# The last head group of an attention kernel gets a program of its own

## The chip, the cores and the metric

The kernel runs on one core of a Trainium2 chip. Five engines work at the same time, each with its own instruction stream, taken in order: TensorE (PE, matrix products), VectorE (DVE), ScalarE (ACT, activation functions), GpSimd (POOL) and SyncE (SP, which here issues every transfer). They are ordered against each other by semaphores alone. The metric is the device time of one execution in microseconds (us); the median of several runs is compared. The profile's span runs from the first to the last instruction of one profiled execution.

## The reference

The inputs are x of 8 x 1024 x 256, four 256 x 256 attention weights and three integer feed-forward weights of hidden size 768. With 16 heads of width 16:

```
xn = layernorm(x)
Q, K, V = xn wq, xn wk, xn wv          # 16 heads; rope on Q and K
probs = softmax(causal(Q K^T / sqrt(16)))
s = (probs V) wo
g = silu(ffn(xn, w_gate, w_up, w_down))
out = x + s * g
```

## The kernel before

The program has two phases. The first (some 480 us) computes Q, K, V and the gate g for all batches and puts them in memory. The second, attention, is what the change touches. It goes over 8 batches b and NG = 4 groups g of GH = 4 heads: 32 steps (b, g). The Python loop writes every step out, and a step is one period of a hand-written order, so that step n works on three things at once: the exponentials of step n, the maxima of steps n+1 and n+2, and the output tiles of a batch that is finished.

- Scores (`keys_by_queries`, L1189 in the trace): NU = 20 units u, each two banks of scores for one block of 128 keys; `EXPU` lists key block, first query, width and heads. ACT makes the exponential of each (`exponentials`, L1110) into one of four buffers `pr`. POOL zeroes the part above the diagonal for the 12 units in `diag_units` (`mask`, L974).
- `times_v(step, s)` (L1207): 12 products s of probabilities and V, four for the first half of the queries (c = 0), eight for the second. Products 9 to 11 (`late`) of a step are run in the period of the next. ACT copies each half of the result out (`take_output`, L1117), PE transposes it (`transpose_output`, L1227), and DVE divides by the row sums (`normalise`, L1060 and L1062) into `an`.
- Maxima (`queries_by_keys`, L1167 and L1175, and `maximum` on DVE, L1029). The last period has none, and that before it only those of the last step.
- Output tiles: 128 queries of a batch by 256, eight to a batch (QB). For each, POOL splits `an` into two half-precision parts (`split_tile`, L982 and L984), PE transposes them (`transpose_tile`, L1235), ACT takes them to `aT` (`take_tile`, L1122), PE multiplies by wo (`project_tile`, L1243, six products), ACT takes the result (`take_product`, L1128), and POOL multiplies by the gate and adds x (`add_tile`, L992 and L995). A full period does two tiles, through one bank, M0.

`ps` is the eight banks of PSUM: three slots of two banks for scores and maxima (`SLOTS`), one bank O0 for the products with V, and M0. `ORDER` is a string of 39 turns of PE; an E is a score unit, an M a unit of maxima, and turn t uses slot t mod 3 (`slot_of`, `wait_slot`). The tuples `V_AT`, `TR`, `WO`, `OUT0`, `OUT1` say behind which turn PE does the rest; `TAKE0`, `TAKE1`, `EV`, `MUL` do so for ACT, `HALVE` and `ADD` for POOL, by units.

When the 32 periods are over, nine tiles are left: the last of batch 6 and all eight of batch 7 (`last_tiles`). They are done in a drain with the three slots as banks:

```
for i in range(len(last_tiles)):
    if i + 1 < len(last_tiles):
        next_tile(i + 1)
    project_tile(last_tiles[i], slot_of(i))
```

and on POOL `split_tile(tile)` of tile i ahead of `add_tile` of tile i - 1, with two buffers each of `ah`, `aT`, `ws` and `yt`. The outputs are stored half a batch at a time (`store_output`, L920).

## Time and profile before

| | us |
|---|---|
| median of 3 runs | 1345.32 |
| lowest, highest | 1344.83, 1348.05 |
| the profiled execution | 1345.25 |
| its span | 1342.8 |
| the last period, first score to last product with V | 26.3 |
| from there to the end of the last division | 3.3 |
| the drain of the tiles | 41.2 |
| the last store | 3.5 |

Over the whole span PE is busy for 92%, DVE for 75%, ACT for 66% and POOL for 46%. These shares hide the end: in the slices of the span PE reads 9 nearly everywhere, and 6 and 3 in the last two. A tuned steady state and a short drain with a limit of its own have to be read apart, so the table cuts the end into stretches. The three stages at the end take 71 us of 1343.

### The profile page before, as it was taken

The page shows a single profiled execution, that of the slowest core. Times are in us where ns is not written, and L with a number is a line of the kernel's source. Part 1 is how long each engine was busy: PE and PEld are TensorE (multiplying, and loading weights), DVE is VectorE, ACT ScalarE, POOL GpSimd, SP SyncE. Part 2 cuts the span into 40 slices and gives each one's busy share as a digit, 9 for nine tenths or more (in the row PEclk, how much of TensorE's full clock was granted, in tenths as well). Part 3 has the DMA queues.
Part 4 walks back from the last instruction along what each step waited for, and adds up shares of the span by engine and source line. Part 5 has one row for each costly group of instructions (what it writes and reads, how often), then busy time and mean ns, then how long its engine had stood idle before and what let it go on. Part 6 is the DMA issues. An engine that isn't in the chain of part 4 may idle for free.

```text
span 1342.8 us, 31209 instructions
## 1 busy us (share of the span) xinstructions
PE 1236.8 (92%) x10999; PEld 579.8 (43%) x10999; DVE 1006.1 (75%) x1217; ACT 890.0 (66%) x1172; POOL 616.7 (46%) x891
## 2 busy tenths in 40 slices
PE   4999999999997699999999999999999999999963
PEld 3556566566564233333333334333333433333321
DVE  5766766666655888888888888888889889888400
ACT  3465564555553177678778877877887787888751
POOL 2664655656664112234444444344444434444444
PEclk8999999999998599999999999999999999999985
DMA  5243343333425211331332333323314313322210
GB/s 211 95 157 111 114 150 125 118 132 125 148 91 160 57 42 41 92 91 43 94 88 76 88 77 92 89 62 106 88 42 112 103 42 103 79 75 65 64 48 31
DMA packets 118388, 125.09 MB, mean 93 GB/s; under 512 B 10880, under 2 KB 103552, under 8 KB 118144
## 3 DMA queue, kind: packets, MB, share of 16 engines
q1 hardware_dynamic: 118272, 123.51, 30.4%
q8 instruction: 77, 1.26, 0.4%
q14 instruction: 39, 0.32, 0.1%
HBM read 72.61 MB, written 50.33 MB: 92 GB/s over the span
## 4 chain that ended last, share of the span: by engine, by line
PE 52%; DVE 7%; ACT 4%; issue 3%; POOL 2%; DMA 0%; SPq 0%; POOLq 0%; ACTq 0%; DVEq 0%
PE ps L1207 20%; PE ps L1189 12%; PE ps L1167 9%; DVE mxp L1029 6%; PE ps L1243 4%; ACT pr L1110 3%; PE ps L1227 3%; PE ps L1175 2%; PE ps L1235 1%; PE ps L1214 1%; DVE mneg L1042 1%; POOL yt L992 1%; POOL ah L984 1%; DMA qs<-mp 0%; POOL zt L995 0%
## 5 line engine op out<-in xcount | busy, mean ns | idle before, releaser
L1029 DVE TENSOR_REDUCE mxp<-ps 128x2 f32<-128x1024 f32 (+2 forms) x576 | 681.4, 1221 | 62.1 <-PE ps L1175 46.0
L1110 ACT ACTIVATE pr<-ps 128x1024 f32<-128x1024 f32 (+2 forms) x640 | 583.4, 938 | 196.5 <-PE ps L1189 189.5
L974 POOL TENSOR_SCALAR_AFFINE_SELECT pr<-pr 128x256 f32<-128x256 f32 (+1 forms) x384 | 188.7, 492 | 421.7 <-ACT pr L1110 421.4
L1207 PE MATMUL ps<-pr,vt 128*32 128x512 f32 (+3 forms) x3072 | 325.7, 505 | 0.3 <-ACT ot L1117 0.2
L1167 PE MATMUL ps<-ks,qs 48*128 48x512 f16 (+2 forms) x1792 | 231.4, 310 | 29.2 <-ACT pr L1110 11.1
L1189 PE MATMUL ps<-qs,ks 50*128 50x512 f16 (+3 forms) x1536 | 236.7, 331 | 18.1 <-DVE mxp L1029 13.9
L1189 PEld LDWEIGHTS ps<-qs,ks 50*128 50x128 f16 x1536 | 70.4, 93 | 246.4 <-issue 239.9
L653 PE MATMUL ps<-xTh,wguT 128*128 128x512 f16 x384 | 145.6, 379 | 0.0
L653 PE MATMUL ps<-xTl,wguT 128*128 128x512 f16 x384 | 145.5, 379 | 0.0
L1167 PEld LDWEIGHTS ps<-ks,qs 48*128 48x128 f16 x1792 | 85.5, 95 | 116.1 <-issue 103.1
L471 DVE SCALAR_TENSOR_TENSOR h<-ps,sg 128x512 f32<-128x512 f32 x96 | 66.1, 690 | 69.1 <-ACT sg L564 53.6
L1207 PEld LDWEIGHTS ps<-pr,vt 128*32 128x32 f32 x3072 | 64.4, 108 | 85.8 <-issue 75.2
L462 DVE TENSOR_TENSOR rot<-ps,trig 128x1024 f32<-128x1024 f32 x64 | 75.4, 1220 | 22.2 <-PE ps L632 22.2
L1175 PE MATMUL ps<-future,pick 64*128 64x128 bf16 (+3 forms) x1024 | 88.7, 248 | 0.0
L564 ACT ACTIVATE sg<-ps 128x512 f32<-128x512 f32 x96 | 57.3, 597 | 41.6 <-PE ps L653 38.9
L551 ACT ACTIVATE parts<-rr 128x1024 f16<-128x1024 f32 x32 | 33.7, 1053 | 76.5 <-POOL rr L523 76.4
L992 POOL TENSOR_TENSOR yt<-ws,gt 128x256 f32<-128x256 f32 x64 | 46.4, 725 | 81.8 <-ACT ws L1128 81.8
L441 POOL TENSOR_TENSOR hl<-h,hh 128x512 f16<-128x512 f32 x64 | 72.8, 1158 | 22.8 <-ACT hh L570 22.8
L632 PE MATMUL ps<-xTh,wqkT 128*128 128x512 f16 x256 | 79.7, 383 | 1.3 <-ACT xTh L546 1.3
L523 POOL TENSOR_TENSOR rr<-rot 128x1024 f32<-128x1024 f32 x32 | 75.4, 2359 | 8.1 <-DVE rot L462 7.4
L570 ACT ACTIVATE hh<-h 128x512 f16<-128x512 f32 x96 | 58.2, 623 | 4.2 <-DVE h L471 4.0
L1175 PEld LDWEIGHTS ps<-future,pick 64*128 64x128 bf16 x1024 | 51.6, 97 | 21.3 <-issue 2.5
(109 smaller groups left out, 1349.0 us busy)
## 6 DMA issues: line engine op xcount, KB each, us to landing
v_d<-vs SPq DMA_DIRECT2D x16, 1024.0 KB, 4.9
vt<-v_d SPq DMA_DIRECT2D x32, 512.0 KB, 4.0
xs<-in_L_attn_x SPq DMA_DIRECT2D x16, 512.0 KB, 4.2
q_parts_d<-parts SPq DMA_DIRECT2D x16, 512.0 KB, 2.9
k_parts_d<-parts SPq DMA_DIRECT2D x16, 512.0 KB, 2.9
gate_d<-gs SPq DMA_DIRECT2D x16, 512.0 KB, 3.2
qs<-q_parts_d SPq DMA_DIRECT2D x64, 128.0 KB, 3.2
ks<-k_parts_d SPq DMA_DIRECT2D x64, 128.0 KB, 3.2
```

The source lines that it names most:

```text
L441: eng.tensor_tensor(hl[:, m], h32[:, m % NH], hh[:, m], ALU.subtract).then_inc((lo_pool if m < LOW_POOL else lo_dve).sem, 1)
L462: ins = dve.tensor_tensor(tq[i][:, t], ps[:, (Q0, K0)[i]:(Q0, K0)[i] + 2, :], trig[:, t, :, c * CH:(c + 1) * CH], ALU.mult)
L523: pool.tensor_tensor(rr[i][:, :, :], tq[i][:, :, 0, :], tq[i][:, :, 1, :], ALU.add).then_inc(rot_add.sem, 1)
L632: ins = pe.matmul(ps[:, (Q0, K0)[i] + eo, :], wqkT[:, wp, kd, 2 * i + eo, :], xx[:, kd, :], start=n == 0, stop=n == len(terms) - 1)
L653: ins = pe.matmul(ps[:, FFN[m] + gu, :], wguT[:, gu, kd, m * P:(m + 1) * P], xx[:, kd, :], start=n == 0, stop=n == 2 * KD - 1)
L974: pool.affine_select(out=blk, in_=blk, compare_op=ALU.is_ge, fill=0.0, base=0, pattern=[[0, 2], [0, len(hs)], [1, P]], channel_multiplier= ...
L1029: dve.tensor_reduce(dst, ps[:, slot:slot + 2, :].rearrange("p t (n s) -> p (t n) s", s=w), axis=AX.X, op=ALU.max).then_inc(max_dve.sem, 1)
L1110: act.activation(pr[s % PROBS].rearrange("p (t j) s -> p t j s", t=2)[:, :, hs[0]:hs[-1] + 1, 0:w], ps[:, slot:slot + 2, 0:w * len(hs)].re ...
L1167: ins = pe.matmul(ps[:, slot + t, n * w:(n + 1) * w], qs[g][r, j, qb * P:(qb + 1) * P], ks[g][r, j, lo:lo + w], start=n == 0, stop=not any ...
L1175: ins = pe.matmul(o, pick[r, half ^ t, :], future[r, half ^ t, 0:len(pieces), half * TILE:P], start=False, stop=half == 1, skip_group_chec ...
L1189: ins = pe.matmul(ps[:, slot + t, n * w:(n + 1) * w], ks[g][r, j, kb * P:(kb + 1) * P], qs[g][r, j, lo:lo + w], start=n == 0, stop=True, s ...
L1207: ins = pe.matmul(ps[VW * j:VW * (j + 1), O0, lo:CH], vt[g % 2][:, kb, j, :], pr[s % PROBS][:, j, 0:CH - lo], start=kb == 0, stop=kb == (c ...
```

## The change

The last step (`LAST`) gets its own program on every engine, `last_group`, in place of a period with empty turns.

- PSUM: the score units use two slots (`score_slot`) and seven output tiles the two banks of the third (`tile_bank`). The seven are the three that are left of batch 6 and the first four of batch 7, whose half (c = 0) of the last step is divided in the middle of the program. New tables say where PE does the products (`V_LAST`), the tiles' transposes (`TR_LAST`) and their projections (`WO_LAST`), and where POOL splits and adds (`HALVE_LAST`, `ADD_LAST`).
- In the last step DVE takes the transposes from PSUM (`take_tile`) and multiplies the projection by scale and gate in one instruction (`gate_product`); ACT does no work for tiles, and POOL only splits and adds.
- Four tiles (`end_tiles`) are left. DVE splits them, PE transposes and projects each in a bank of its own, ACT takes the transposes, DVE makes the products, and POOL and DVE add two each. Each is stored alone.
- `ah`, `aT`, `ws`, `yt` have four buffers (`TILES`).

```diff
@@ tables and slots
+            last_tiles = [(B - 2, t) for t in range(2 * (NG - 1) - 1, QB)] + [(B - 1, t) for t in range(CT)]
+            end_tiles = [(B - 1, t) for t in range(CT, QB)]
+
+            def score_slot(step, u):
+
+                return 2 * (u % 2) if step == LAST else slot_of(E_TURN[u])
+
+            def tile_bank(i):
+
+                return 2 * (SLOTS - 1) + i % 2
...
+            V_BEFORE, V_LAST = (0, 1, 1), (3, 5, 6, 7, 9, 11, 13, 15, 17, 19, NU, NU)
@@ sync, behind the periods
-                for c in range(HALVES):
-                    store_output(B - 1, c)
+                store_output(B - 1, 0)
+                for i, (b, t) in enumerate(end_tiles):
+                    sp.wait_ge(s_end[i % 2], i // 2 + 1)
+                    sp.dma_start(out_v[b, 1][:, t % CT], zt[:, 1, t % CT]).then_inc(s_stored, 16)
@@ gpsimd
-                for i, tile in enumerate(last_tiles):
-                    split_tile(tile)
-                    if i:
-                        add_tile(last_tiles[i - 1])
-                add_tile(last_tiles[-1])
+                def last_group(step, prev):
+                    split_tile(last_tiles[0])
+                    for u in range(NU):
+                        if u in diag_units:
+                            mask(step, diag_units.index(u))
+                        for i, tile in enumerate(last_tiles):
+                            if u == HALVE_LAST[i]:
+                                split_tile(tile)
+                            if u == ADD_LAST[i]:
+                                add_gated(tile).then_inc(t_add.sem, 1)
@@ vector
+                def take_tile(tile, bank):
+                    wait(dve, t_ev, earlier(tile, 1))
+                    wait(dve, t_wo, earlier(tile, TILES))
+                    wait(dve, t_tr, tile)
+                    dve.tensor_copy(aT[:, tile[1] % TILES].rearrange("p l k t -> p (l k t)"),
+                                    ps[:, bank, 0:D].bitcast(F16)).then_inc(t_ev.sem, 1)
+                def gate_product(tile, bank):
...
+                    wait(dve, t_wo, tile)
+                    dve.scalar_tensor_tensor(out=yt[:, t % TILES], in0=ps[:, bank, D:2 * D], scalar=oscale[:, 0:1], in1=gt[:, c, t % CT],
+                                             op0=ALU.mult, op1=ALU.mult).then_inc(t_mul.sem, 1)
...
+                for tile in end_tiles:
+                    split_tile(tile)
+                for i, tile in enumerate(end_tiles):
+                    b, t = tile
+                    gate_product(tile, i)
+                    if i % 2:
...
+                        dve.tensor_tensor(zt[:, 1, t % CT], yt[:, t % TILES], xt[:, 1, t % CT], ALU.add).then_inc(s_end[1], 1)
@@ scalar
+                    for u in range(NU):
+                        exponentials(step, u)
+                        if u == TAKE1_LAST:
+                            take_output(prev, 1)
+                        if u == TAKE0_LAST:
+                            take_output(step, 0)
+                    take_output(step, 1)
...
+                for i, tile in enumerate(end_tiles):
+                    wait(act, t_ev, earlier(tile, 1))
+                    take_tile(tile, i)
@@ tensor, keys_by_queries
-                    wait_slot(pe, step, E_TURN[u])
+                    if step != LAST:
+                        wait_slot(pe, step, E_TURN[u])
+                    elif u < 2:
+                        wait_slot(pe, step, u)
+                    else:
+                        wait(pe, expo, step, u - 1)
@@ tensor
+                        for i, tile in enumerate(last_tiles):
+                            if u == TR_LAST[i]:
+                                if i < 2:
+                                    wait_slot(pe, step, SLOTS - 1)
+                                else:
+                                    wait(pe, t_mul, last_tiles[i - 2])
+                                transpose_tile(tile, tile_bank(i))
+                            if u == WO_LAST[i]:
+                                project_tile(tile, tile_bank(i))
...
+                wait(pe, expo, LAST)
+                for i, tile in enumerate(end_tiles):
+                    transpose_tile(tile, i)
+                    if i:
+                        project_tile(end_tiles[i - 1], i - 1)
+                project_tile(end_tiles[-1], len(end_tiles) - 1)
```

PE in the middle of the last step. `qs,ks` are scores, `pr,vt` products with V, `identh,ah` a tile's transposes, `woT,aT` its projection, `ident,ot` the transposes of a half of the attention output. Before, from unit 13 on:

```order
L1189 MATMUL ps<-qs,ks 128x512 x4
L1207 MATMUL ps<-pr,vt 32x512 x4
L1189 MATMUL ps<-qs,ks 128x512 x2
L1189 MATMUL ps<-qs,ks 128x384 x2
L1235 MATMUL ps<-identh,ah 128x128 x4
L1189 MATMUL ps<-qs,ks 128x384 x2
L1243 MATMUL ps<-woT,aT 128x256 x6
L1189 MATMUL ps<-qs,ks 128x256 x4
L1207 MATMUL ps<-pr,vt 32x512 x4
```

After, from unit 12 on:

```order
L1298 MATMUL ps<-qs,ks 128x512 x2
L1344 MATMUL ps<-identh,ah 128x128 x4
L1298 MATMUL ps<-qs,ks 128x512 x2
L1316 MATMUL ps<-pr,vt 32x512 x4
L1344 MATMUL ps<-identh,ah 128x128 x4
L1298 MATMUL ps<-qs,ks 128x512 x2
L1352 MATMUL ps<-woT,aT 128x256 x6
L1298 MATMUL ps<-qs,ks 128x512 x2
L1316 MATMUL ps<-pr,vt 32x512 x4
L1352 MATMUL ps<-woT,aT 128x256 x6
```

Where one tile stood among the last eight score units, there are now four, each in two pieces: its transposes, and later its projection, between score units and products with V.

PE at the end, from the last products with V. Before (the two rows of transposes and projection then repeat for each tile):

```order
L1207 MATMUL ps<-pr,vt 32x256 x4
L1207 MATMUL ps<-pr,vt 32x128 x4
L1235 MATMUL ps<-identh,ah 128x128 x4
L1227 MATMUL ps<-ident,ot 128x128 x4
L1235 MATMUL ps<-identh,ah 128x128 x4
L1243 MATMUL ps<-woT,aT 128x256 x6
```

After, complete but for the closing branch:

```order
L1316 MATMUL ps<-pr,vt 32x256 x4
L1316 MATMUL ps<-pr,vt 32x128 x4
L1336 MATMUL ps<-ident,ot 128x128 x4
L1344 MATMUL ps<-identh,ah 128x128 x8
L1352 MATMUL ps<-woT,aT 128x256 x6
L1344 MATMUL ps<-identh,ah 128x128 x4
L1352 MATMUL ps<-woT,aT 128x256 x6
L1344 MATMUL ps<-identh,ah 128x128 x4
L1352 MATMUL ps<-woT,aT 128x256 x12
```

Nine tiles stood behind the last product; four stand there now, all of them behind the transposes of the last half.

DVE at the end, after, from the take of the sixth and seventh tile (before, DVE's stream ended with RECIPROCAL and TENSOR_TENSOR an). `rec` and `an` are the division:

```order
L1131 COPY aT<-ps 128x512 x2
L1142 SCALAR_TENSOR_TENSOR yt<-ps,oscale,gt 128x256 x2
L1099 RECIPROCAL rec<-ps 128x16
L1101 TENSOR_TENSOR an<-ps,rec 128x4x64
L1151 CAST ah<-an 128x256
L1153 TENSOR_TENSOR ah<-an,ah 128x256
```

The splits of the four end tiles, which POOL did, stand right behind the division on the same engine; the pair of split rows repeats three more times.

## Rows read from the trace of the kernel before

**Rows 1.** The page: its span, and TensorE's granted clock in 40 slices.

```profile
span 1342.8 us, 31209 instructions
PEclk8999999999998599999999999999999999999985
```

**Rows 2.** Stretches: length, busy PE, PEld, DVE, ACT, POOL, clock, DMA share, GB/s.

```profile
1268.50:1294.80 26.30, 21.84 (x199) 7.14 (x196) 1.36 (x4) 20.08 (x26) 12.41 (x23) 0.94 0.19 60
...
1298.10:1339.30 41.20, 14.03 (x80) 8.39 (x77) 0.00 (x0) 7.45 (x17) 20.23 (x32) 0.56 0.16 51
1339.30:1342.80 3.50, 0.00 (x0) 0.00 (x0) 0.00 (x0) 0.00 (x0) 0.03 (x1) 0.50 0.43 150
```

**Rows 3.** Timeline of PE, last step: start, us, line, instructions [idle before <-releaser].

```profile
1268.51 0.39 PE L1189 MATMUL ps<-qs,ks 50*128 50x512 f16 x2
1268.84 0.85 PE L1207 MATMUL ps<-pr,vt 128*32 128x384 f32 x8
1269.62 0.39 PE L1189 MATMUL ps<-qs,ks 50*128 50x512 f16 x2
...
1272.26 0.38 PE L1235 MATMUL ps<-identh,ah 128*128 128x128 f16 x4 [1.41 <-POOL ah L984]
1272.58 0.34 PE L1189 MATMUL ps<-qs,ks 50*128 50x384 f16 x2
1272.84 0.43 PE L1207 MATMUL ps<-pr,vt 128*32 128x128 f32 x8
1273.40 0.83 PE L1243 MATMUL ps<-woT,aT 128*128 128x256 f16 x6
...
1274.63 1.07 PE L1207 MATMUL ps<-pr,vt 128*32 128x512 f32 x8
...
1278.78 0.66 PE L1227 MATMUL ps<-ident,ot 128*128 128x128 f32 x4 [0.43 <-ACT ws L1128]
...
1289.75 1.94 PE L1207 MATMUL ps<-pr,vt 128*32 128x512 f32 x8
```

**Rows 4.** Timeline of POOL and of ACT, last step.

```profile
1270.57 0.42 POOL L974 TENSOR_SCALAR_AFFINE_SELECT pr<-pr 128x256 f32<-128x256 f32 x1
```

```profile
1289.92 1.02 ACT L1110 ACTIVATE pr<-ps 128x1024 f32<-128x1024 f32 x1
...
1294.95 0.60 ACT L1117 ACTIVATE ot<-ps 128x512 f32<-128x512 f32 x1 [2.23 <-PE ps L1207]
```

**Rows 5.** Timeline of all engines, end of the drain.

```profile
1329.97 0.72 POOL L992 TENSOR_TENSOR yt<-ws,gt 128x256 f32<-128x256 f32 x1 [2.58 <-ACT ws L1128]
...
1331.52 0.40 POOL L982 TENSOR_SCALAR ah<-an 128x256 f16<-128x256 f32 x1
1332.01 0.67 POOL L984 TENSOR_TENSOR ah<-an,ah 128x256 f16<-128x256 f32 x1
...
1332.82 0.58 PE L1235 MATMUL ps<-identh,ah 128*128 128x128 f16 x4 [3.42 <-POOL ah L984]
...
1333.20 1.48 PE L1243 MATMUL ps<-woT,aT 128*128 128x256 f16 x6
...
1335.25 0.72 POOL L992 TENSOR_TENSOR yt<-ws,gt 128x256 f32<-128x256 f32 x1 [2.58 <-ACT ws L1128]
...
1338.61 0.72 POOL L995 TENSOR_TENSOR zt<-yt,xt 128x256 f32<-128x256 f32 x1
1339.36 0.38 SPq L920 DMA_DIRECT2D out_dram<-zt  x1
```

**Rows 6.** Groups of DVE instructions by form: count, busy us, mean ns, idle before.

```profile
L433 DVE TENSOR_TENSOR parts<-rr,parts 128x1024 f16<-128x1024 f32 x16 | 38.9, 2433 | 18.4 <-ACT parts L551 18.4
L1062 DVE TENSOR_TENSOR an<-ps,rec 128x256 f32<-128x256 f32 x64 | 27.2, 425 | 2.2
...
L441 DVE TENSOR_TENSOR hl<-h,hh 128x512 f16<-128x512 f32 x32 | 22.0, 687 | 1.6
...
L453 DVE COPY xTl<-ps 128x1024 f16<-128x1024 f16 x16 | 11.0, 685 | 2.4 <-PE ps L616 2.4
```

More of the change, by code:

```diff
@@ L765, in attention_phase @@
         zt = sb("zt", [P, HALVES, CT, D], F32)
[L766 to L768 removed]
+        ws = sb("ws", [P, TILES, D], F32)
+        yt = sb("yt", [P, TILES, D], F32)
+        aT = sb("aT", [P, TILES, 2, KD, P], F16)
         s_held = sem("s_held2")
         s_cl = sem("s_cl")
+        s_end = [sem(f"s_end{i}") for i in range(2)]
+        s_stored = sem("s_stored")
         s_unfilled = sem("s_unfilled")
@@ new lines, in gate_product @@
+                def gate_product(tile, bank):
+                    b, t = tile
+                    c = t // CT
+                    if t % CT == 0 or tile == last_tiles[0]:
+                        dve.wait_ge(o_ld[c], b * 32 + 32)
+                    wait(dve, t_mul, earlier(tile, 1))
+                    wait(dve, t_add, earlier(tile, TILES))
+                    wait(dve, t_wo, tile)
+                    dve.scalar_tensor_tensor(out=yt[:, t % TILES], in0=ps[:, bank, D:2 * D], scalar=oscale[:, 0:1], in1=gt[:, c, t % CT],
+                                             op0=ALU.mult, op1=ALU.mult).then_inc(t_mul.sem, 1)
@@ new lines, in split_tile @@
+                def split_tile(tile):
+                    b, t = tile
+                    src = an[b % 2][:, t]
+                    wait(dve, t_lo, earlier(tile, 1))
+                    wait(dve, t_tr, earlier(tile, TILES))
+                    wait(dve, o_norm, LAST)
+                    dve.tensor_copy(ah[:, t % TILES, 0], src).then_inc(t_hi.sem, 1)
+                    wait(dve, t_hi, tile)
+                    dve.tensor_tensor(ah[:, t % TILES, 1], src, ah[:, t % TILES, 0], ALU.subtract).then_inc(t_lo.sem, 1)
@@ new lines, in last_group @@
+                def last_group(step, prev):
+                    take = lambda i: take_tile(last_tiles[i], tile_bank(i))
+                    product = lambda i: gate_product(last_tiles[i], tile_bank(i))
+                    take(0)
+                    product(0)
+                    normalise(prev, 1)
+                    take(1)
+                    product(1)
+                    take(2)
+                    normalise(step, 0)
+                    product(2)
+                    take(3)
+                    take(4)
+                    product(3)
+                    product(4)
+                    take(5)
+                    take(6)
+                    product(5)
+                    product(6)
+                    normalise(step, 1)
@@ L1221, in transpose_output @@
                         wait(pe, t_out, tile)
-                    else:
+                    elif ahead(step, 1):
                         wait(pe, mx_neg, nth(step, 1))
```

109 lines of the change are left out of this document (61 added, 48 removed).

## The prediction

> **What bounds the kernel now.** I read the page first, for where the end differs from the rest: the granted clock is full (9) in the attention slices and 8 and 5 in the last two [rows 1]. Then the end cut into stretches [rows 2]. In the last step PE is busy 21.84 of 26.30 us. In the drain of nine tiles it is busy 14.03 of 41.20 us, POOL 20.23, DVE never: no engine is full there, so a chain bounds it. The timeline of one tile shows the chain [rows 5]: POOL starts a multiplication by the gate at 1329.97 and the next at 1335.25, so a tile costs 5.28 us. In between POOL adds, splits the next tile but one (from 1331.52 to 1332.68), PE transposes (to 1333.40) and projects (to 1334.68), ACT takes the product, POOL goes on. POOL is at both ends of the loop. The projection takes 1.48 us at the lower level of the clock (1.2 GHz), against 0.83 in the last step at the upper one (2.4 GHz) [rows 3, 5]. So what the change is worth is: the drain gone, less what seven tiles add to the last step, less a new end of four tiles. Steps before the last keep their order and are left out of the sum.
>
> **PE's work in the new last step.** PE's next instruction starts 0.07 us before the modelled end of a product with V (1268.84 + 0.85 against 1269.62), so a product with V of 512, 384, 256, 128 columns occupies PE 1.00, 0.78, 0.57, 0.36 us (0.57 is midway between the rows of 384 and 128), and a score ahead of it 0.33, of which I book 0.23 to the score and 0.10 to the product [rows 3]. The 20 scores: 14 of 0.23, four of 0.19 and two of 0.12 (shares of 0.23 by columns), 4.2 us. The step's 12 products: 6 x 1.10 + 2 x 0.88 + 2 x 0.67 + 2 x 0.46 = 10.6. The three carried over from the step before: 0.88 + 0.67 + 0.36 = 1.9. Seven transposes at 0.32 (1272.26 to 1272.58) are 2.2; seven projections at 0.76 (0.83 less 0.07) are 5.3; two transposes of an output half at 0.59 (0.66 less 0.07) are 1.2 [rows 3]. The sum is 25.4 us, against 21.84 busy in the row, a dip of the clock included [rows 2]: PE is nearly full, and no other engine comes near it. ACT needs 14 x 0.92 + 4 x 0.70 + 2 x 0.50 for exponentials (one of 1.02 hands over 0.10 early; the shorter ones are estimates by columns) and 3 x 0.5 for copies, 18.2 us [rows 4]: it is hidden. Two slots instead of three cost nothing while that holds: score u waits for exponential u - 2, and PE always has other work longer than an exponential between them.
>
> **Waits of PE in it.** I followed the tables from 1268.51, with 0.10 us from PE's end to another engine and 0.15 from another engine to PE (1332.68 to 1332.82 in [rows 5]). PE stands where: (a) the first transpose waits for POOL's split, which can start when POOL is free at 1270.57 [rows 4] and takes 0.48 + 0.67 [rows 5], so until 1271.87, 0.9 us; (b) the first product with V waits for ACT's copy of the carried half, 0.3; (c) the fifth waits for ACT's copy of the first half, which stands behind exponential 8, 1.3; (d) the transpose of the fourth tile waits for a split that POOL starts only behind the third tile's addition, and that one waits for DVE's product of it: projection ready at 1283.9, product 1284.5, addition 1285.3, split 1286.4, so 1.1; (e) the product with key block 6 waits for a mask that stands behind an addition on POOL, 0.4. Together 4.0 us. Everything else that is added is covered by PE: DVE's take of 512 half-precision values from PSUM is 0.42 us if it goes like the copy of 1024 of them in 0.685, or 0.69 if like 512 values in the row of 0.687 [rows 6], and a score or product lies between most transposes and their projections; if that cover were gone it would cost 7 x 0.27 = 1.9. DVE's product by the gate is 0.425. POOL's seven splits (1.15 each), seven additions and 12 masks are some 18 us of 29.
>
> So the last product with V ends at 1268.5 + 25.4 + 4.0 = 1297.9, where before it ended at 1294.8: plus 3.1 us. That before holds a drop of the clock, one product at 1.94 instead of 1.07 [rows 3], which my 25.4 leaves out. From there: ACT's copy (0.10 + 0.60 + 0.14, [rows 4]), PE's transposes 0.66, DVE's division 0.10 + 0.29 + 0.42, in all 2.3: division done at 1300.3. Before it was done at 1298.1, since 41.2 us of drain started there. **Cost of the last step: 2.2 us.**
>
> **The new end.** From the division: DVE splits a tile in a cast and a subtraction. The cast is between 0.28 (at the rate of the copy of 1024 in 0.685) and 0.425. The subtraction is between 0.42 (512 in 0.687 have the same kinds of operands, and 256 from PSUM take 0.425) and 0.61 (a quarter of the 2.43 that 1024 took in the dearer row) [rows 6]. I take 0.28 and 0.42, the latter since its row is nearest in size and kinds. With 0.03 between them a tile is 0.73 and the fourth split is done at 2.9 us. Its transpose waits behind the others' work on PE to 3.9; ACT takes it (0.10 + 0.60 + 0.14) at 5.2, and projection (0.83), product (0.10 + 0.42) and DVE's addition (0.42, with the two hand-overs) end at **7.0** at the full clock. At half clock throughout, projections being 1.36 apart instead of 0.76 (1.48 and 0.83 with the same overlap), the same walk ends at **9.9**. In the drain of before the mean clock was 0.56, so it fell early in it [rows 2], and the new end is sparse on PE from the last product on: I take 9.2, with only the first projection at full clock. Subtractions of 0.61 would add some 0.4. Additions on POOL (0.72) end before DVE's last and cost nothing.
>
> The last store: from the end of the last addition, 1339.33, to 1342.8, 3.5 us [rows 2, 5] for half a megabyte; now it is 128 KB behind three like it. I take 3.3, between 2.5 and 3.7.
>
> The Trainium skill, page DMA: Bandwidth & Descriptors, section Anatomy of one DMA, puts a transfer at about 2.0 us fixed plus bytes over 436 GB/s, measured there on GpSimd's path. By it the end would be some 2.3 us and the total 1.0 lower; by the row it is 3.3. No run so far shows a store of 128 KB.
>
> **Sum.** New end of span: 1300.3 + 9.2 + 3.3 = 1312.8, against 1342.8: minus 30.0 us. In parts: plus 2.2 for the last step, minus 41.2 plus 9.2 for tiles behind it, minus 0.2 for the store. The profiled execution took 1345.25 in all, 2.45 outside the span, and is 0.07 from the median of 1345.32. So 1345.3 - 30.0 = **1315.3 us**.
>
> **Rivals.**
> 1. The clock falls inside the last step. It did before, though PE was busy for 21.84 of 26.30 us: mean 0.94 in the step [rows 2], and a product at 1.94 us [rows 3]. Against it speaks that PE now has 25.4 of 29.4 us of work. The 0.94 of 26.3 us are 3.2 us at the lower level, so 1.6 us of work lost; one or two such stretches give plus 1.6 to 3.2: 1316.9 to 1318.5. The Trainium skill, page TensorE: Matmul & The Clock Gate, section Part 1, says "the default state is throttled, and activity releases the throttle". By that rule rival 1 needs a stretch in which PE does little; the drop at 1289 agrees, and the waits (c) and (d) are where it could come again.
> 2. The clock stays full through the new end: 9.2 becomes 7.0, so 1313.1. For it: only 10 us pass between the last dense work and the end. Against: half clock in nearly the whole drain before.
> 3. The end keeps the drain's pace. If the four tiles do not overlap, they come 5.28 apart: 3 x 5.28 plus one chain from split to addition (1331.52 to 1339.33, 7.8) are 23.7 instead of 9.2: 1329.8. Against it: each tile has its own bank and buffers, and no engine has both ends of the chain before another tile's start.
> 4. Slower than before: the tiles starve the last step. PE is in order and stands at each transpose for DVE's product two tiles back and at each projection for DVE's take; DVE in turn is in order. If each of seven tiles held PE for a full round of 5.28, that is 37.0, and PE, thin again, ran its other 18 us of work at half clock, 36: 73 us in place of 29.4, plus 43.6, 1358.9. It decides from 34 us of PE waits in the step, where the gain of 30 is used up; I count 4.0. For it speaks only that the round of 5.28 exists in rows; against it that DVE has nothing else to do and takes 0.4 where POOL took 0.7 and more.
> 5. The change doesn't do what it says, because the drain was hidden by something else and the end comes as late as now. Then the time stays at 1345.3. But POOL's last addition ends at 1339.33 and the last store is issued at 1339.36 [rows 5], so the drain is on the end, and I give this next to nothing.
>
> **How the numbers follow.** Forecast 0.58, rival 1 0.18, rival 2 0.16, rival 3 0.04, rival 4 0.02, rival 5 and anything else near no change 0.02. The range goes down to rival 2 with 1.0 less for the store and 0.6 less waits (1311.5), and up to rival 1 with the dearer subtractions (0.4) and 1.1 us more of waits (1320.0); it leaves out rivals 3 to 5 and the tails of the others, some 2 in 10. A measurement of this kernel can tell 0.3%, 4 us. Faster by more: forecast and rivals 1 to 3, less a little, 0.96. Within: 0.02. Slower: 0.02.
>
> **What would show it.** Right: PE busy above 24 us in the some 29 from the first score of the last step to its last product with V; no wait of PE over 1.5 us there, and the largest for ACT's copy and for POOL's fourth split; 2.2 to 2.4 us from there to the division; the last addition 7 to 10 us later; last projections at about 1.4 us. Wrong: waits in the last step of over 6 us in sum (rival 4's beginning), a granted clock under 0.95 in it (rival 1), full clock to the end (rival 2), or tiles 5 us apart at the end (rival 3). A last store of under 3 us would move the sum by itself. If earlier steps changed their period of about 26 us, the whole argument would miss it.

## The result, and the profile after

The changed kernel takes 1310.99 us (median of 4 runs, 1309.08 to 1311.97), the kernel before, beside it, 1345.07: a ratio of 0.9745, 95% interval 0.972 to 0.9769. That is 34.1 us less, where 30.0 were forecast, and 0.5 us below the low end of the range, 1311.5. Timed again in another set (`after_again`), the median is 1311.56, just inside the range, the ratio 0.9751 [0.9729, 0.9773] and the difference 33.0 us.

The page of the profiled execution (1309.08 us in all, so 1.78 outside the span), for [rows 1]. It was the shortest of the four runs:

```profile
span 1307.3 us, 31201 instructions
PEclk8999999999999589999999999999999999999999
```

The last two digits were 8 and 5 and are 9 and 9: the end at half clock is nearly gone. The same stretches as in [rows 2]: the last step to its last product with V; from there to the division; the new end; the store.

```profile
core 0: us, PE busy (x) PEld busy (x) DVE busy (x) ACT busy (x) POOL busy (x), PEclk, DMA share, GB/s
1264.70:1294.30 29.60, 26.06 (x250) 10.54 (x246) 7.62 (x18) 19.38 (x22) 19.59 (x36) 1.00 0.34 107
1294.30:1296.65 2.35, 0.66 (x8) 0.42 (x4) 0.68 (x2) 0.60 (x1) 0.24 (x1) 1.00 0.49 168
1296.65:1305.10 8.45, 5.85 (x40) 4.13 (x40) 5.66 (x14) 2.39 (x4) 1.44 (x2) 0.80 0.15 48
1305.10:1307.30 2.20, 0.00 (x0) 0.00 (x0) 0.00 (x1) 0.00 (x0) 0.00 (x0) 1.00 0.35 119
```

Where 41.2 us stood with PE at 14.03 busy, there are 8.45 with PE at 5.85 and DVE at 5.66. The step of 26.3 us has become one of 29.6 in which PE is busy for 26.06, at full clock throughout.

PE's waits of over 0.2 us in that step, from its timeline (the columns of [rows 3]); they stand in the order of the prediction's (a) to (e):

```profile
1268.11 0.38 PE L1344 MATMUL ps<-identh,ah 128*128 128x128 f16 x4 [0.81 <-POOL ah L1009]
...
1268.96 1.07 PE L1316 MATMUL ps<-pr,vt 128*32 128x512 f32 x8 [0.21 <-POOL pr L999]
...
1277.20 1.06 PE L1316 MATMUL ps<-pr,vt 128*32 128x512 f32 x8 [1.02 <-ACT ot L1213]
...
1282.70 0.38 PE L1344 MATMUL ps<-identh,ah 128*128 128x128 f16 x4 [1.12 <-POOL ah L1009]
...
1293.31 1.01 PE L1316 MATMUL ps<-pr,vt 128*32 128x256 f32 x16 [0.38 <-POOL pr L999]
```

They sum to 3.5 us. The new end, from the timeline of all engines, for [rows 5]:

```profile
1297.11 0.43 DVE L1153 TENSOR_TENSOR ah<-an,ah 128x256 f16<-128x256 f32 x1
...
1298.84 1.46 PE L1352 MATMUL ps<-woT,aT 128*128 128x256 f16 x6
...
1300.52 1.49 PE L1352 MATMUL ps<-woT,aT 128*128 128x256 f16 x6
...
1302.23 1.79 PE L1352 MATMUL ps<-woT,aT 128*128 128x256 f16 x12
...
1304.16 0.48 DVE L1142 SCALAR_TENSOR_TENSOR yt<-ps,oscale,gt 128x256 f32<-128x256 f32 x1 [0.46 <-PE ps L1352]
1304.68 0.42 DVE L1185 TENSOR_TENSOR zt<-yt,xt 128x256 f32<-128x256 f32 x1
```

The first two projections run at the lower level of the clock (1.46 and 1.49 us), the third and fourth share a row of 1.79 us for twelve products, so some 0.9 each: the upper level is back by then. DVE still waits 0.46 us for the fourth. The tiles are 1 to 1.7 us apart and no longer 5.28.

### The profile page after: what moved, and what is told of

It is laid out like the page before. It is cut to its first block, busy times and chain, and to the rows that moved or that the text cites. A ratio compares the mean times of both kernels' runs of the same rounds, so it can differ in the third digit from the quotient of the medians.

```text
span 1307.3 us, 31201 instructions
## 1 busy us (share of the span) xinstructions
PE 1228.1 (94%) x10999; PEld 577.1 (44%) x10999; DVE 1018.0 (78%) x1245; ACT 883.5 (68%) x1154; POOL 603.0 (46%) x870
## 4 chain that ended last, share of the span: by engine, by line
PE 53%; DVE 7%; ACT 3%; issue 2%; DMA 1%; POOL 0%; SPq 0%; DVEq 0%; ACTq 0%; POOLq 0%
PE ps L1316 21%; PE ps L1298 13%; PE ps L1271 9%; DVE mxp L1068 6%; PE ps L1352 3%; PE ps L1336 3%; PE ps L1279 2%; ACT pr L1206 2%; PE ps L1344 1%; DMA qs<-mp 1%; PE ps L1323 1%; DVE mneg L1081 1%; SPq L923 0%; ACT aT L1218 0%; POOL pr L999 0%
## 5 line engine op out<-in xcount | busy, mean ns | idle before, releaser
L1316 PE MATMUL ps<-pr,vt 128*32 128x512 f32 (+3 forms) x3072 | 321.5, 498 | 1.6 <-ACT ot L1213 1.0
L1271 PE MATMUL ps<-ks,qs 48*128 48x512 f16 (+2 forms) x1792 | 230.9, 310 | 28.4 <-ACT pr L1206 10.9
L1024 POOL TENSOR_TENSOR yt<-ws,gt 128x256 f32<-128x256 f32 x53 | 38.4, 725 | 60.6 <-ACT ws L1224 60.6
```

The lines of the kernel that those rows point to most:

```text
L1271: ins = pe.matmul(ps[:, slot + t, n * w:(n + 1) * w], qs[g][r, j, qb * P:(qb + 1) * P], ks[g][r, j, lo:lo + w], start=n == 0, stop=not any ...
L1316: ins = pe.matmul(ps[VW * j:VW * (j + 1), O0, lo:CH], vt[g % 2][:, kb, j, :], pr[s % PROBS][:, j, 0:CH - lo], start=kb == 0, stop=kb == (c ...
```

## Experiments

Letters in an expectation are the theories of that run alone. "Ratio" is always to the kernel before, run on the same chip in the same set; the medians of before lay between 1344.6 and 1345.9 us.

### Both kernels unchanged

> The kernel before, unchanged, once more. The last step began 3.8 us earlier in the profile of after (first score at 1264.74) than in that of before (1268.51), though the steps ahead of it hold the same instructions. Theory A (chance of the clock: before's profile shows four short drops of the granted clock between 480 and 570 us, after's none, so 3.8 us of the distance of the two profiles is luck of a run): this run's first score of the last step lies anywhere from 1264.5 to 1270, spans of repeated runs spread by 3 us or more, and a longer span goes with a lower mean clock. Theory B (the change makes the earlier steps faster, by other addresses of the buffers): the first score of the last step is again at 1268 or later, and the drops at 480 to 570 are there again. Both: ratio to before 1.000 within 0.15%; about 2.45 us of the device time lie outside the span, as in the first profile (in after it was 1.78).

> The changed kernel, unchanged, once more, for a second profile and a closer ratio. My account of the first profile of after, from the first score of the last step to the end of the span, is 42.6 us against 74.3 in before, so 31.7 us, and 0.7 less outside the span: 32.4. Theory A (the rest of the measured 34.1 is luck of the runs): over more rounds the difference of the medians is 31.5 to 33.5 us, ratio 0.9751 to 0.9766, and the first score of the last step is not always at 1264.7. Theory B (earlier steps are faster by 3.8 us for good): difference 35 to 37 us, ratio 0.9725 to 0.974.

The kernel before against itself gave 1345.08 (12 runs, 1342.08 to 1350.19), ratio 1.0004 [0.9989, 1.0019]; the changed one 1311.56 (5 runs, 1310.04 to 1314.73). In the profile of after the last step had started at 1264.7, 3.8 us earlier than before the change, though the order of the steps ahead of it was not changed (only their tile buffers are four now, not two). The new profiles say that this is not the change's doing: the first score of the last step came at 1266.2 with the kernel before, and at 1270.0 with the changed one. Nor do the buffers matter: from DVE's negation of the maxima near 637 us (the row is shown below, for earlier steps) to the first score of the last step all four profiles take 629.6 to 629.8 us, so the difference lies ahead of it. The granted clock in the first attention steps tells them apart. Stretches of before, of after and of `after_again`, in this order:

```profile
480.00:490.00 10.00, 8.74 (x72) 2.69 (x68) 7.73 (x9) 5.61 (x7) 3.59 (x8) 0.83 0.17 48
...
560.00:570.00 10.00, 8.69 (x76) 2.80 (x72) 8.46 (x9) 5.24 (x7) 3.86 (x9) 0.83 0.24 61
```

```profile
480.00:490.00 10.00, 8.69 (x84) 2.87 (x80) 9.15 (x10) 6.68 (x9) 4.01 (x9) 1.00 0.29 65
...
560.00:570.00 10.00, 9.48 (x94) 3.01 (x94) 9.80 (x9) 6.80 (x9) 3.40 (x8) 1.00 0.41 88
```

```profile
480.00:490.00 10.00, 8.74 (x76) 2.64 (x70) 7.75 (x9) 6.00 (x7) 3.61 (x8) 0.83 0.09 23
...
560.00:570.00 10.00, 8.69 (x72) 2.81 (x68) 7.76 (x8) 5.53 (x8) 3.60 (x8) 0.83 0.11 29
```

What a dip costs is read from an instruction that comes once in a step, DVE's negation of the maxima. Its rows in before and in after:

```profile
480.92 0.28 DVE L1042 TENSOR_SCALAR mneg<-ps 32x128 f32<-32x128 f32 x1 [0.65 <-PE ps L1214]
...
507.66 0.28 DVE L1042 TENSOR_SCALAR mneg<-ps 32x128 f32<-32x128 f32 x1 [0.65 <-PE ps L1214]
```

```profile
481.19 0.28 DVE L1081 TENSOR_SCALAR mneg<-ps 32x128 f32<-32x128 f32 x1 [0.65 <-PE ps L1323]
...
506.50 0.28 DVE L1081 TENSOR_SCALAR mneg<-ps 32x128 f32<-32x128 f32 x1 [0.65 <-PE ps L1323]
```

The step took 26.7 us with the dip and 25.3 without. Over four such steps it is 25.2 to 25.4 without one and 26.7 to 27.0 with one: 1.4 to 1.6 us each, step against like step, here and not there from run to run of the same kernel. There are three in the profiles of before and `after_again`, two in `old_end`, one in `before_again` and `share_only`, none in after. So 3.8 us of the difference between the two profiles are luck; and of the difference between two medians of few runs, a us or so may be, which no run here separates.

### The last store

One store of 512 KB behind all four additions, where there are four of 128 KB.

```diff
-for i, (b, t) in enumerate(end_tiles):
-    sp.wait_ge(s_end[i % 2], i // 2 + 1)
-    sp.dma_start(out_v[b, 1][:, t % CT], zt[:, 1, t % CT]).then_inc(s_stored, 16)
+for e in s_end:
+    sp.wait_ge(e, 2)
+sp.dma_start(out_v[B - 1, 1], zt[:, 1]).then_inc(s_stored, 16)
```

> After, but the last four tiles are stored with one transfer of half a megabyte behind the last addition, as before did, in place of four of 128 KB each behind its own addition. I had 3.3 us from the last addition to the end of the span; after shows 2.2, before 3.5. Theory A (the size of what is left to move sets that stretch): it goes back to 3.3 to 3.6, and the 0.7 us outside the span go back to 2.4 as well if they hang on the same transfer; time plus 1.1 to 1.8 us against after. Theory B (2.2 and 3.5 differ for another reason, as other engines being idle): stretch stays at 2.0 to 2.5 and time within 0.5 us of after.

Measured: 1312.47 (1312.26 to 1316.25), ratio 0.9765 [0.9743, 0.9788], not told from after by its interval; the median is 0.9 us above that of `after_again` in the same set. The stretch tells it: from the last addition to the end of the span,

```profile
1310.10:1313.60 3.50, 0.00 (x0) 0.00 (x0) 0.01 (x1) 0.00 (x0) 0.00 (x0) 1.00 0.44 150
```

3.5 us, as before the change for the same 512 KB, against 2.2 and 2.4 us in the two profiles of after. The time outside the span stayed at 1.7 us, so that does not hang on the store's size. The lists of transfers (size, median time from issue to landing) say the same of the transfer itself, before and after:

```profile
out_dram<-zt SPq DMA_DIRECT2D x16, 512.0 KB, 3.6
...
qs<-mp SPq DMA_DIRECT2D x128, 4.0 KB, 1.7
```

```profile
out_dram<-zt SPq DMA_DIRECT2D x4, 128.0 KB, 1.7
```

The last store of the kernel before took 2.9 us from issue to landing.

### One part at a time

`share_only` is the kernel before with its own last period of two tiles; the nine tiles behind it are drained as the change drains four (DVE splits, DVE products, additions in turn on POOL and DVE, four buffers). Here and for `old_end` only POOL's part of the edit is shown, and here the list of tiles.

```diff
+end_tiles = [(B - 2, QB - 1)] + [(B - 1, t) for t in range(QB)]
+over_groups(group, None)
+for i, tile in enumerate(end_tiles):
+    if i % 2 == 0:
+        add_gated(tile).then_inc(s_end[0], 1)
```

> One part of the change alone: the last step keeps the period of before with its two tiles, nine tiles are left as before, but they are drained by all engines as the four are in after (DVE splits and multiplies by the gate, ACT takes the transposes, POOL and DVE add every other one, four buffers and banks, the last half batch stored tile by tile). In after the tiles at the end are 1.7 us apart (projections at 1298.84, 1300.52, 1302.23), and 8.45 us pass from the division to the last addition of four. Theory A (sharing is the larger part, and the tiles then cost what PE and DVE take for one): last step 26.3 us as before; from the division to the last addition 8.45 + 5 x 1.7 = 17 us, up to 18.5 since the gate and x of the last half are loaded behind the first tile; time 24 to 26 us below before, so some 8 us above after. Theory B (moving five tiles into the last step is what pays): the nine tiles are still 4 us or more apart, time less than 12 us below before.

`old_end` is after's last step, with its four end tiles drained as before.

```diff
 for i, tile in enumerate(end_tiles):
-    if i % 2 == 0:
-        add_gated(tile).then_inc(s_end[0], 1)
+    split_tile(tile)
+    if i:
+        old_add(i - 1, end_tiles[i - 1])
+old_add(3, end_tiles[3])
```

> The other part alone: after's last step with its seven tiles and two slots, but the four tiles of the end go through the old chain (POOL splits, multiplies by the gate and adds; ACT takes transposes and products), with after's banks, buffers and single stores. My rival 3 priced this pace at 3 x 5.28 + 7.8 = 23.7 us from the division to the last addition, against 8.45 in after. Theory A: 21 to 24 us there, time 13 to 15 us above after, the last step unchanged at 29.6 us. Theory B (the old chain was slow for its two buffers and three banks, not for POOL at both its ends): 12 to 16 us there, time 4 to 8 us above after. On the time outside the span (1.8 us in after, 2.45 in most runs of before): if it hangs on the four single stores or on after's program it is 1.8 here, if on a long thin drain it is 2.4.

Measured: `share_only` 1316.62 (1316.04 to 1317.29), ratio 0.9787 [0.9768, 0.9805]; `old_end` 1323.02 (1320.31 to 1324.22), ratio 0.9827 [0.9806, 0.9848]. From the last division to the last addition, in this order:

```profile
1296.32:1312.27 15.95, 10.70 (x90) 7.70 (x90) 13.18 (x32) 5.37 (x9) 3.62 (x5) 0.89 0.47 152
```

```profile
1300.48:1320.16 19.68, 7.71 (x40) 4.57 (x40) 0.01 (x1) 3.60 (x8) 10.02 (x16) 0.52 0.08 27
```

Nine tiles shared cost 16 us (41.2 before), four by the old chain 19.7. Both are less than theory A's ranges (17 to 18.5, and 21 to 24), and so are both times: `share_only` is 28.4 us below before, where 24 to 26 were expected, and `old_end` some 12 above after, where it was 13 to 15. In `old_end` POOL's multiplications by the gate start at 1305.62, 1310.85 and 1316.08, the old period of 5.2 with four tiles as with nine. The chain of the last tile, from its split to its addition (1312.40 to 1320.16), is the 7.8 us of rival 3. What rival 3 had wrong is the 3 x 5.28 ahead of it: POOL splits the second tile right behind the first, 1.3 us apart, and only from then on are the splits 5.2 to 5.3 apart:

```profile
1300.58 0.41 POOL L1009 TENSOR_SCALAR ah<-an 128x256 f16<-128x256 f32 x1 [2.20 <-DVE an L1114]
...
1301.88 0.41 POOL L1009 TENSOR_SCALAR ah<-an 128x256 f16<-128x256 f32 x1
...
1307.17 0.41 POOL L1009 TENSOR_SCALAR ah<-an 128x256 f16<-128x256 f32 x1
```

Each part alone takes 28 and 22 us off, and both together 33 to 34: they remove the same drain. Sharing it among the engines is the larger part; moving five more tiles into the last step brings the last 5 us.

### What bounds the last step

`project_one` makes one of a tile's six products with wo in the seven tiles of the last step; the other five are left out, so these tiles' outputs are partial.

```diff
 if u == WO_LAST[i]:
-    project_tile(tile, tile_bank(i))
+    wait(pe, t_ev, tile)
+    pe.matmul(ps[:, tile_bank(i), D:2 * D], aT[:, tile[1] % TILES, 0, 0, :], woT[:, 0, 0, :],
+              start=True, stop=True).then_inc(t_wo.sem, 1)
```

> After, but each of the seven tiles in the last step is projected with one product instead of six, so PE has 7 x 0.63 = 4.4 us less work there (the output of these tiles is then one sixth of the projection's terms, a part of the computation left out). In after the step takes 29.6 us from first score to last product with V. Theory A (PE bounds the step, but for the waits I counted): following the tables with the shorter projections the waits for POOL and for ACT grow by 1.9 us, so the step takes 27.1 us, between 26.5 and 28. Theory B (chains through DVE, ACT and POOL bound it, PE's idle is only misplaced): 29 us or more. Theory C (PE alone): 25.2.

The step lasted 26.8 us in the one run there is (theory A had 27.1). The time that PE gives a projection fell from 0.76 to 0.21, 3.9 in seven, and the waits grew from 3.5 to some 4.4 (three of about 1: 1.18 for POOL's split, 0.92 for ACT's copy, 0.93 for a mask). So PE's own work bounds the step, and a little of the saved work turns into waits.

`tuned` moves three entries of the tables, against waits (c), (d) and (e): ACT copies the half one exponential earlier, and two additions of POOL go behind a split and a mask.

```diff
-OUT1_LAST, OUT0_LAST, TAKE1_LAST, TAKE0_LAST = 4, 9, 2, 8
-HALVE_LAST, ADD_LAST = (-1, 1, 5, 11, 11, 12, 13), (6, 8, 10, 14, 15, 17, 19)
+OUT1_LAST, OUT0_LAST, TAKE1_LAST, TAKE0_LAST = 4, 9, 2, 7
+HALVE_LAST, ADD_LAST = (-1, 1, 5, 11, 11, 12, 13), (6, 8, 12, 14, 15, 19, 19)
```

> After, with three numbers of its tables changed, to try the waits that I counted on PE in the last step: ACT copies the first half behind exponential 7, not 8; POOL adds the third tile behind the splits of the fourth and fifth, not ahead of them; POOL adds the sixth tile behind the mask of the last unit. Theory A (those waits are on the path: 1.02 us before the fifth product with V, 1.12 before the fourth tile's transposes, 0.38 before the product with key block 6): all three fall below 0.3 us, the last step from first score to last product with V goes from 29.6 to 27.0 to 27.8 us, and the time falls by 1.8 to 2.6 us against after. Theory B (another wait, ACT's exponentials with two slots, comes right behind them): the waits only move, and the step stays above 28.8 us, the time within 0.8 us of after.

Measured: 1308.44 (1306.85 to 1310.29), ratio 0.9727 [0.9706, 0.9749], 3.1 us below `after_again` in the same set, though the two intervals overlap. The step:

```profile
1268.85:1295.58 26.73, 25.69 (x247) 10.59 (x246) 7.63 (x18) 19.18 (x22) 19.22 (x36) 1.00 0.39 118
```

26.7 us in place of 29.6, PE busy for 25.7 of them; none of the three waits is left in PE's timeline. So they were on the path, as the prediction said, and could be removed without a new one. The three are 2.5 us; PE's own busy time fell by another 0.4, from 26.06 to 25.69, so the step came out below the 27.0 to 27.8 expected. Where the 0.4 come from is open.

`two_slots` gives the kernel before two slots for the scores of its last step, and nothing else.

```diff
-slot = slot_of(E_TURN[u])
+slot = slot_of(E_TURN[u]) if step != (B - 1, NG - 1) else 2 * (u % 2)
```

> Before, with one thing of the change: in the last step the scores go through two slots instead of three (the third is left unused until the drain). Nothing else moves. Step in before: 26.3 us from first score to last product with V. Theory A (a slot comes free before PE is back with a score, since an exponential is 0.92 us and other work lies between): step 26.0 to 27.0 us, time within 0.7 us of before. Theory B (ACT in turn with PE is the limit of this thin step, and the third slot covered it): 28 us or more, time plus 2 to 4 us; then after would have paid this as well, hidden in my sum of PE's waits.

1345.82 (10 runs), ratio 1.0006 [0.9993, 1.0018], the step 26.3 us as before: the third slot was worth nothing there. In the fuller step of after the trace shows no wait of PE for an exponential of over 0.2 us either.

### The clock at the end and at the start

`tuned_busy` is `tuned` with 12 products that nobody reads, on PE, behind the last product with V: they fill the time in which PE waits for ACT's copy, the division and the splits.

```diff
+wait(pe, t_mul, last_tiles[-2])
+keep_busy(3, tile_bank(5))
 transpose_output(step, 1)
+keep_busy(8, tile_bank(5))
...
 transpose_tile(tile, i)
+if i == 0:
+    keep_busy(1, tile_bank(5))
```

> The tuned tables of the run tuned, and PE kept at work at the end by twelve products whose result nobody reads (identity by wo, 512 columns, 0.22 us each at the full clock, into a bank that is free): three between the last product with V and the transposes of the last half, eight behind these, one between the first two tiles. In tuned the first two projections of the end run at the lower level of the clock (1.41 and 1.49 us for six products, tiles 1.7 us apart), the last ones at the upper, and 8.5 us pass from the division to the last addition; PE does next to nothing in the 4 us ahead. Theory A (the clock of the end is set by PE's idling there and is on the path): all transposes and projections at 0.40 and 0.83 us, tiles 1.1 us apart, 6.6 to 7.4 us from division to last addition, as my walk at the full clock gave 7.0; time 1.2 to 2 us below tuned's 1308.4. Theory B (DVE's four splits, 3.1 us, bound the end whatever the clock is): 8 us or more, time as tuned.

Measured: 1306.51 (1305.98 to 1309.29), ratio 0.9713 [0.9699, 0.9728], the best here; its interval overlaps that of `tuned`. From the division to the last addition, and PE in it:

```profile
1295.12:1301.94 6.82, 5.39 (x46) 3.35 (x43) 5.58 (x15) 2.39 (x4) 1.45 (x2) 1.00 0.25 85
```

```profile
1294.14 1.89 PE L1366 MATMUL ps<-woT,identh 128*128 128x512 f16 x8
...
1297.32 0.83 PE L1352 MATMUL ps<-woT,aT 128*128 128x256 f16 x6
...
1298.21 0.82 PE L1352 MATMUL ps<-woT,aT 128*128 128x256 f16 x6
...
1299.14 1.71 PE L1352 MATMUL ps<-woT,aT 128*128 128x256 f16 x12
```

All projections are at the upper level, and the end takes 6.8 us against 8.4 in `tuned`: the clock's part of the end is 1.6 us. The Trainium skill, page TensorE: Matmul & The Clock Gate, section Part 1, has it that activity releases the throttle. These rows agree in so far as the clock stayed up where PE was kept at work, and the activity need not be of use.

`both_split` adds to it that POOL splits the second and fourth end tile while DVE splits the first and third (POOL's part is shown).

```diff
+if i % 2:
+    pool.tensor_scalar(ah[:, t % TILES, 0], an[b % 2][:, t], 1.0, 0.0, ALU.mult, ALU.add).then_inc(s_hx[1], 1)
+    pool.tensor_tensor(ah[:, t % TILES, 1], an[b % 2][:, t], ah[:, t % TILES, 0], ALU.subtract).then_inc(s_lx[1], 1)
```

> tuned_busy, but POOL splits the second and the fourth tile of the end while DVE splits the first and the third. In the drain that shared nine tiles a subtraction on DVE took 0.92 us whenever an addition on POOL ran at its side (at 1301.00, 1304.06, 1307.12) and 0.42 otherwise. Theory A (these two engines get in each other's way when both read two tensors from SBUF): DVE's subtractions beside POOL's splits take 0.7 us or more, the fourth tile is ready at 2.8 us or later behind the division, as when DVE splits alone (3.2), and the time is within 0.6 us of tuned_busy. Theory B (0.92 was a chance of that place): DVE 0.42 and POOL 0.67 side by side, all four ready at 2.3 to 2.5 us, end 0.6 to 0.9 us shorter.

1307.76 (1306.43 to 1310.88), ratio 0.9719 [0.9703, 0.9736], 6.86 us from the division to the last addition: no gain. The two engines do slow each other, though not where theory A had it: DVE's subtractions took 0.50 us (0.42 alone), but its second cast, the second row here, took 0.76 where 0.29 is usual:

```profile
1299.08 0.71 POOL L1061 TENSOR_TENSOR ah<-an,ah 128x256 f16<-128x256 f32 x1
1299.19 0.76 DVE L1189 CAST ah<-an 128x256 f16<-128x256 f32 x1
```

That is not why there was no gain. The fourth tile was split 2.7 us behind the division, between the two theories and 0.6 ahead of `tuned_busy` (3.25). But the first projection starts 2.2 us behind the division in both runs, and from there PE's transposes and projections set the pace: DVE's four products by the gate are 0.9 us apart in both, the first at 3.2 and the last at 5.9. So at full clock the splits of the later tiles are not on the path.

`busy_start` is `tuned_busy` with three unread products for each absent tile in the first five attention steps.

```diff
+if n == WO[i] and not tiles[i]:
+    wait(pe, mx_neg, nth(step, i))
+    keep_busy(3, M0)
```

> tuned_busy, and in the first five steps of attention, which have no or one output tile, three such unread products stand where a tile's projection would stand. Every profile so far but one shows drops of the granted clock at about 484, 512 and 562 us, in just these steps, and the first score of the last step came at 1264.7 in the one profile that had none, at 1266.2 to 1270.0 in the others. Theory A (the spread of the runs, and some 2 us of the distance between a lucky profile and the median, is these drops, and they come because PE is thin there): granted clock 1.00 from 490 to 580 us in the profile, spans within 2.5 us of each other in place of 4 to 5, median 1 to 3 us below tuned_busy. Theory B (the drops hang on something else, or the products cost as much as they save since PE is busy for 93% there): drops still there, or median the same or higher by up to 2 us.

1308.60 (1307.58 to 1309.63), ratio 0.9724 [0.9711, 0.9737], which overlaps the interval of `tuned_busy`. The clock was 1.00 from 480 to 620 us, but so it was in the profile of `tuned_busy`, which has no filling there; the five runs lie within 2.1 us, those of `tuned_busy` within 3.3. That the filling takes the dips away is therefore not shown. What it costs is shown: four of the filled steps took 25.9 to 26.2 us, against 25.2 to 25.4 at full clock without it. From 481 us on, six periods took 156.2 us, where they are 154.0 in `tuned_busy` and 157.9 in before, with its three dips. And some 2 us more were lost behind them, 0.2 to 0.6 in one step of every four, where no unread product stands. Why is open, so the 2.1 us between the two medians are not the price of the filling alone.

## Where the prediction held and where it failed

The mechanism held: the drain went, at the price of a fuller last step and a short end. Sizes failed. The step that failed most is the price of the last store, 3.3 us and at least 2.5, where 2.2 to 2.4 were measured. Beside it the new end was priced 0.75 us too high, and two terms stood at nothing without a reason: the time outside the span, which fell by 0.7, and the spread of the steps ahead of the last.

The difference of the two profiled executions, 1345.25 - 1309.08 = 36.2 us, term by term:

| term | predicted | measured |
|---|---|---|
| steps ahead of the last | 0 | -3.8 |
| last step, to the end of the division | +2.2 | +2.35 |
| the drain | -41.2 | -41.2 |
| the new end | +9.2 | +8.45 |
| the store | -0.2 | -1.3 |
| outside the span | 0 | -0.7 |
| sum | -30.0 | -36.2 |

- **The last step** held, by two misses that nearly cancel. From its first score to the last product with V it took 29.6 us, where 29.4 were worked out: 26.1 of work for 25.4, and 3.5 of waits for 4.0. The missing work is in the scores. Each took 0.32 (at 1283.01, 1284.66 and 1285.74), but only those with a product with V behind them were booked in full; the sum had 5.6 us for the twenty, and they are 6.3. The waits came where the tables had been walked: (a) 0.81 for 0.9, (b) 0.21 for 0.3, (c) 1.02 for 1.3, (d) 1.12 for 1.1, (e) 0.38 for 0.4. Of (b) the trace names a mask of POOL as what ended it, not ACT's copy. `tuned` shows (c) to (e) for what they were, `project_one` that the rest is PE's work, `two_slots` that two slots cost nothing in the step of before.
- **From V to the division**: 2.35 for 2.3.
- **The new end** is the first term that was mis-sized, by 0.75 us. The forecast had the clock fall behind the first projection and stay low; it was low for the first two and high for the last two. In four profiles (after, `after_again`, `one_store`, `tuned`) it took 8.4 to 8.7. That lies between the forecast and rival 2, 7.0 us at full clock, which `tuned_busy` bears out with 6.8. The bounds of 7.0 and 9.9 held the 8.45. The cast took 0.29 and the subtraction 0.42 (0.28 and 0.42 were taken).
- **The store** is the second and the largest, by 1.1 us: 2.2 us (2.4 in `after_again`) against 3.3, and below my bound of 2.5. I had stayed near one row, 3.5 us for 512 KB. `one_store` shows that what is left to move behind the last addition is the whole cause: with 512 KB it is 3.5 again. The trace before had more to go by, the 1.7 us from issue to landing of its 4 KB transfers against 2.9 of its last store; a line between the two gives an estimate of 2.0 for 128 KB, 0.9 less than for 512. The estimate from the Trainium skill, page DMA: Bandwidth & Descriptors, section Anatomy of one DMA, 2.3 us, was the better price for the stretch. That is in part luck, since from issue to landing these stores took only 1.7.
- **Outside the span** is the third, by 0.7 us, and had no bounds at all. It was 2.45 in the one execution of before and 1.78 in that of after. Over all sets it was 1.7 to 3.1 us with the kernel before, and 1.7 to 1.9 with every kernel that has after's last step. What it consists of stays open: it does not hang on the last store's size, and `share_only`, with the old last period and the new stores, had 1.9 to 2.6.
- **The steps ahead of the last** kept their order, and their time changed by luck: 3.8 us between the two profiles. A median of three or four runs can carry some of it. The forecast was made against a profile with three dips, and the one profile of after in its set has none; how many the other three runs had is not on record (their mean clocks of 0.975 to 0.978 lie between that of the profile without a dip, 0.979, and that of `after_again` with three, 0.974).

The three mis-sized terms are 2.5 us, all in one direction, and with them the sum gives 1312.8, inside the range. The remaining 1.8 us to 1310.99 are within what runs of one kernel differ by, and the early dips are the likely part of it, which is argued and not shown; with `after_again`, 0.6 of them are gone. The range was too narrow since it added only the store and a little of the waits to rival 2, and left the outside of the span and the dips out. Of the rivals, rival 1 did not come (clock 1.00 in the last step), rival 2 came by a third (0.75 of 2.2 us), 3 to 5 did not; `old_end` prices rival 3 at 1323.0, where it had said 1329.8. Of the prediction's own signs, a last store of under 3 us came, and the last projections were not at 1.4 us.

## What to carry to other kernels

Read the drain behind a full steady state by itself: here 41 us in which no engine was half busy came down to 16 by giving the nine tiles to all engines, before any was moved. Count a new stage by its order tables, wait by wait: that was right to 0.2 us in 29.6 (by misses of 0.7 and 0.5 against each other) and named the three entries that were worth another 2.9 in the step. Give bounds also to what seems not to change, the last store's size, the time outside the span and the dips of the clock, and compare medians of two sets before explaining a difference of 2 us.

## Of the hardware, not expected

- **DVE and POOL at once.** DVE's subtraction of 256 values, 0.42 us alone, took 0.92 in `share_only` each of the three times that an addition on POOL had started just ahead of it:

```profile
1303.97 0.72 POOL L1018 TENSOR_TENSOR zt<-yt,xt 128x256 f32<-128x256 f32 x1 [2.34 <-DVE yt L1193]
1304.06 0.92 DVE L1155 TENSOR_TENSOR ah<-an,ah 128x256 f16<-128x256 f32 x1
...
1306.07 0.42 DVE L1155 TENSOR_TENSOR ah<-an,ah 128x256 f16<-128x256 f32 x1
```

POOL's own time stays at 0.72, and DVE ends 0.3 us after it. The cast of `both_split` above ends 0.16 us after POOL's subtraction. It goes the other way too: POOL's cast there, begun 0.06 us behind DVE's at 1298.44, took 0.50 where it is 0.41 alone. The Trainium skill, page SBUF — State Buffer, section SBUF: two separate sides, calls the port pair that the two share an exclusive lock, taken by whoever starts first. The rows agree in who is held up and in that it ends behind the other; they don't show it held completely, since a subtraction begun only at POOL's end would have ended 0.42 us after it, not 0.3. In the changed kernel's end the one addition on POOL that falls beside a DVE product from PSUM (1303.84 and 1304.16) leaves it at its 0.48.

- **The clock** came back to its upper level inside the new end, in which PE was busy for 5.85 of 8.45 us. In `share_only` the first 4.7 us of the drain have a mean of 0.64 and the rest 1.00:

```profile
1296.32:1301.00 4.68, 3.48 (x22) 2.48 (x23) 3.56 (x12) 1.52 (x3) 0.09 (x1) 0.64 0.00 0
1301.00:1312.27 11.27, 7.22 (x70) 5.21 (x68) 9.61 (x21) 3.85 (x7) 3.53 (x5) 1.00 0.66 215
```

In the drain before, with PE at 14.03 of 41.20, the mean had stayed at 0.56 [rows 2]. So a denser end got part of the clock back by itself here, which the forecast did not count on.
- **Dips in nearly full steps.** PE is busy for 93% of 470 to 620 us, but not evenly. Before and after, each in the same two stretches:

```profile
481.00:484.00 3.00, 1.74 (x24) 0.89 (x22) 3.00 (x4) 2.12 (x3) 1.77 (x6) 1.00 0.02 4
484.00:488.00 4.00, 4.00 (x30) 0.89 (x28) 2.58 (x3) 1.62 (x2) 1.31 (x3) 0.57 0.06 11
```

```profile
481.00:484.00 3.00, 1.74 (x21) 0.91 (x22) 2.81 (x4) 2.32 (x3) 1.90 (x5) 1.00 0.01 3
484.00:488.00 4.00, 3.95 (x38) 1.15 (x38) 3.80 (x4) 1.70 (x4) 1.69 (x3) 1.00 0.23 59
```

In both PE is busy for 1.74 of 3 us. Behind that the clock falls in one profile and not in the other, so the thin stretch alone does not decide it. The drop in the last step of before also follows one: PE busy for 1.40 us from 1286 to 1289, then a mean clock of 0.66 to 1294.
